# Turning the contexts between the thirds of the next pair's scores

## The reference

```python
# layer 0 (one head of width 8, its output repeated for 16 heads)
q = query @ Wq + bq; k = key @ Wk + bk; v = value @ Wv + bv
scores = jnp.einsum('bqd,bkd->bqk', q, k) / math.sqrt(HIDDEN)
scores = _layer_norm_scores(scores)          # mean and std over the 1500 keys
scores = scores + jnp.where(m, -1e-32, 0.0)
attn = jax.nn.softmax(scores, axis=-1)
head = jnp.einsum('bqk,bkd->bqd', attn, v)
return jnp.tile(head, (1, 1, NUM_HEADS)) @ Wout + bout
# layer 3 (layer norms of query, key and value around one head of width 128)
qk = jnp.einsum('bqd,bkd->bqk', q, k)
probs = jax.nn.softmax(qk / inv_scale_factor, axis=2)
out = jnp.einsum('bqk,bkd->bqd', probs, v)
return _layernorm(out, ln4_w, ln4_b)
```

## Time and profile before

| what | value |
|---|---|
| median of 3 runs | 3416.47 us (3416.21 to 3417.08) |
| the profiled execution's own time | 3413.9 us |
| its span in the profile | 3412.1 us |
| mean granted TensorE clock | 0.932 |
| TensorE busy | 3079.0 us, 90% of the span |
| layer 0: round 0 starts, last `out_turned` | 44.12 us, 208.67 us |
| layer 3: round 0 starts, last `out_turned` | 3087.48 us, 3254.01 us |

### The profile page before, as it was taken

The page is one execution under the profiler, slowest core; times in us unless marked ns, Lnnn a source line. Parts: engine busy times, 40 slices in busy tenths (PEclk is TensorE's granted clock), DMA queues, the critical chain, the costliest instruction groups (busy, mean ns, idle before and its releaser), DMA issues. The chain is left out here.

```text
span 3412.1 us, 74955 instructions
## 1 busy us (share of the span) xinstructions
PE 3079.0 (90%) x30282; PEld 2137.9 (63%) x30282; DVE 2292.5 (67%) x4268; ACT 1742.8 (51%) x2862; POOL 1869.8 (55%) x1048
## 2 busy tenths in 40 slices
PE   7979989999999999999979998899999995349969
PEld 5654556777777777777757777455555553236644
DVE  4555557777777777777644443799999985654455
ACT  4534325666656666665644454366666663114545
POOL 0004556777777777777642220588888872014427
PEclk9979988999999999999989999799999996559989
DMA  7730016776666667767514665433333321304600
GB/s 142 145 114 22 1 37 125 139 147 130 134 137 142 130 134 139 142 131 140 111 51 154 235 236 218 98 99 98 96 96 92 92 69 36 55 0 93 135 1 12
DMA packets 607380, 367.70 MB, mean 108 GB/s; under 512 B 462933, under 2 KB 566626, under 8 KB 606786
## 3 DMA queue, kind: packets, MB, share of 16 engines
q1 hardware_dynamic: 607042, 362.96, 46.1%
HBM read 174.41 MB, written 75.24 MB: 73 GB/s over the span
## 5 line engine op out<-in xcount | busy, mean ns | idle before, releaser
L1742 POOL TENSOR_TENSOR L_plo<-L_p,L_phi 128x1500 bf16<-128x1500 f32 x224 | 659.1, 2943 | 295.0 <-DVE L_phi L1819 295.0
L1699 ACT COPY L_ptlo<-L_lt 128x1536 bf16<-128x1536 bf16 x224 | 322.1, 1438 | 407.6 <-PE L_lt L1623 407.6
L2121 ACT ACTIVATE L2b_p<-L2b_score 125x448 f32<-125x448 f32 x768 | 378.7, 541 | 273.2 <-PE L2b_score L2034 272.0
L1637 PE MATMUL L_acc<-L_chi,L_pthi 125*128 125x128 bf16 x2688 | 462.1, 219 | 0.0
L1639 PE MATMUL L_acc<-L_chi,L_ptlo 125*128 125x128 bf16 x2688 | 461.4, 219 | 0.0
L1638 PE MATMUL L_acc<-L_clo,L_pthi 125*128 125x128 bf16 x2688 | 461.2, 219 | 0.0
L1808 DVE TENSOR_SCALAR_CACHE_REDUCE L_p<-L_score,L_cols 128x1500 f32<-128x1500 f32 x224 | 395.4, 1765 | 84.8 <-PE L_score L1615 84.6
L1819 DVE CAST L_phi<-L_p 128x1500 bf16<-128x1500 f32 x224 | 298.1, 1331 | 164.6 <-ACT L_p L1693 163.7
L1693 ACT ACTIVATE L_p<-L_p,L_least 128x1500 f32<-128x1500 f32 x224 | 346.5, 1547 | 67.0 <-DVE L_p L1808 63.1
L2164 POOL TENSOR_TENSOR L2b_psum<-L2b_p 125x896 f32<-125x896 f32 x128 | 266.8, 2084 | 131.0 <-ACT L2b_p L2121 128.6
L2191 DVE TENSOR_REDUCE L2b_max<-L2b_m 112x1 f32<-112x1000 f32 x256 | 300.7, 1195 | 17.2 <-PE L2b_m L2015 9.5
(11 more groups left out here) (635 smaller groups left out, 6890.8 us busy)
## 6 DMA issues: line engine op xcount, KB each, us to landing
L2b_kst<-L_keys SPq DMA_DIRECT2D x96, 375.0 KB, 5.6
L_ct<-L_ct SPq DMA_DIRECT2D x32, 768.0 KB
L2a_ct<-L_ct SPq DMA_DIRECT2D x32, 768.0 KB, 15.1
L_ctx<-dram_ctx SPq DMA_DIRECT2D x32, 750.0 KB
L_keys<-L2a_kout SPq DMA_DIRECT2D x32, 750.0 KB, 8.0
L_values<-L2a_vout SPq DMA_DIRECT2D x32, 750.0 KB
L2b_vin<-L_values SPq DMA_DIRECT2D x32, 750.0 KB
L0x_ctx<-dram_ctx SPq DMA_DIRECT2D x32, 672.0 KB
```

Source lines behind the costliest of these rows:

```text
L1637: pe.matmul(acc, w_hi[0:KP, t, :], v_hi[0:KP, t, :], start=(t == 0), stop=False)
L1699: act.copy(pt_lo[g % 2][:, :, :], lt_ps[:, 0:KT * 128].rearrange("p (t q) -> p t q", t=KT)).then_inc(lo_read, 1)
L1742: pool.tensor_tensor(p_lo[g % 2][:, :, 0:KP], probs[g % RP][:, :].rearrange("q (t k) -> q t k", t=KT), p_hi[g % 2][:, :, 0:KP], ALU.subtra ...
L2121: act.activation(probs[t % RP][:, half * 2 * GW:(half + 1) * 2 * GW], score_ps[half][0:KP, 0:2 * GW], ACT.Exp).then_inc(exp_done, 1)
```

## The change

On TensorE, groups 0, 1 and 2 of pair n+2 no longer stand behind the probabilities of pair n but one behind each third of the scores of pair n+1; group 3 stays where it was. On ScalarE, the copies of these three groups stand ahead of `output(n - 1)`. No instruction is added or taken away, and the order on VectorE, GpSimd and the transfer queue is as before.

```diff
-                def scores(n):
+                def scores(n, thirds):
                     if n >= P:
                         return
                     pe.wait_ge(tr_read, 2 * G * (n + 1))
-                    for i in range(3):
+                    for i in thirds:
                         wait(pe, exp_done, 3 * (n - 1) + i + 1 if n else 0)
...
                 for n in range(P):
-                    scores(n + 1)
+                    for i in range(3):
+                        scores(n + 1, (i,))
+                        turned_keys(n + 2, (i,))
                     if n >= 1:
                         out_turned(n - 1)
                     turned_probs(n, 0)
                     turned_probs(n, 1)
-                    turned_keys(n + 2, (0, 1, 2, 3))
+                    turned_keys(n + 2, (3,))
                     weighted(n, 0)
...
                 for n in range(P):
+                    keys(n + 2, (0, 1, 2))
                     if n >= 1:
                         output(n - 1)
-                    keys(n + 2, (0, 1, 2, 3))
+                    keys(n + 2, (3,))
                     exps(n + 1)
                     keys(n + 2, (4, 5))
```

More of the change, by code:

```diff
@@ L1015, in _ @@
                 pe.wait_ge(q_ready, NCH)
-                scores(0)
+                scores(0, range(3))
                 turned_keys(1, range(2 * G))
```

## The result

The changed kernel takes 3421.34 us (median of 13 runs, 3417.87 to 3428.22) against 3415.51 us for the kernel before in the same comparison (13 runs). The ratio is 1.0019 with a 95% interval of 1.001 to 1.0027: 6.5 us more, 3.4 to 9.2. The forecast was 3420.6, 4.1 us more than the 3416.5 it started from.

The account below looks back on a forecast made before the run. TensorE was taken to set the pace in both stages; layer 0's round +0.33 us and layer 3's -0.04, 14 times each, add 4.1 us to 3416.5, giving 3420.6 us; 8 in 10 between 3414.5 and 3426.0.

Parts of the forecast that it names:

- The copy waits: TensorE's third and fourth context groups wait for ScalarE's copies; 0.54 us a round (layer 0), 0.60 (layer 3), 16 us, go.
- Changeovers: Switching TensorE between half-array scores and whole-array transposes around two inserted context groups adds 0.51 us a round.
- S2: Last third of a round's scores on TensorE; forecast to start 3.05 us after the first third instead of 1.68.
- The lower bound: Changeovers cost only 0.10 us each way there, 0.20 for both inserted groups, if all else hides.
- the upper of 0.74: Changeovers cost 0.37 us each, as between weighted matmuls and transposes, 0.74 for both; rival's chance 0.16.
- The estimate of 0.66 us: Four added changeovers a round at 166 ns each instead of 0.51 us in all; forecast about 4 us higher.
- Layer 0's new wait on VectorE's copy: First weighted matmul waits for transposed probabilities, 3.30 us behind the scores' last third; TensorE idles 0.33 us a round.
- Layer 3 even: Layer 3's shorter VectorE chain adds practically no wait; round 10.69 us, 0.04 less than 10.73.
- Loads: Context transfers stay hidden, in layer 0 with 11.9 us where they had 14.3; late-load rival's chance 0.04.
- The 4.65 us: Stretch from a round's first weighted matmul to the next scores on TensorE, forecast unchanged in both layers.
- The rivals: Upper changeover price 3427.0 us, chance 0.16; no VectorE wait 3416.0, 0.10; hidden changeovers 3411.9, 0.06; late layer 0 loads 3431, 0.04.
- The sum: 14 rounds in each layer, 0.33 us longer in layer 0 and 0.04 shorter in layer 3: 4.1 us more.

Follow-up runs that it names:

- two groups ahead: Kernel before, with the first two groups of transposed contexts ahead of the first two groups of transposed probabilities on TensorE: 3401.69 us, ratio 0.9959.
- the single transpose between thirds: Kernel before, with only the one transpose `out_turned` moved from behind the scores' last third to behind the first: ratio 1.0029, 9.9 us slower.
- alone: The change made in layer 3 only, layer 0 keeping the order of the kernel before: ratio 1.0005.
- either new order on VectorE: Changed kernel, layer 0: first copy of transposed probabilities ahead of the aggregate, 1.0016; second copy also ahead of scale and bias, 1.0012 (ratios).
- one group between: Changed kernel, with one context group between the scores' first two thirds and two groups behind the last third: ratio 0.9983 against the kernel before.
- both copies first: Changed kernel, layer 0: VectorE's first copy of transposed probabilities ahead of the aggregate, the second ahead of scale and bias: ratio 1.0012.
- one block: On top of two groups ahead: all transposes together, then all weighted matmuls; ScalarE copies all six groups before the probabilities: 3381.86 us, ratio 0.9901.

## Why the prediction was right

- *The copy waits go.* Right, and sized right: 0.54 and 0.60 us a round read, 0.56 and 0.62 measured where nothing else changed (two groups ahead).
- *Changeovers.* Right: 0.51 us a round was forecast up to S2, and S2's place, 3.08 - 1.68 - 0.87, gives 0.53. The lower bound, weights hidden beneath the transposes, does not hold, nor does the upper of 0.74. One changeover there and back costs 0.29 us where one is taken out, so two cost 0.58: the 0.53 and about 0.05 behind S2. It is shown apart from everything else by the single transpose between thirds. The Trainium skill's rule (TensorEngine Tiling (Array Packing), Key Properties) that changing the tiling mode drains TensorE fits the gaps, but no run shows the drain itself. The estimate of 0.66 us from the 166 ns of the Trainium skill (TensorE: Matmul & The Clock Gate, Single matmul latency) is above what the rounds show.
- *Layer 0's new wait on VectorE's copy.* Right in place and size: 3.32 behind S2, 3.30 forecast, read off a round of the kernel before that turned no contexts. Round 11.05 for 11.00.
- *Layer 3 even.* 10.70 for 10.69, and alone not to be told from before.
- *Loads, ScalarE, the rest of the round.* The 4.65 us stayed. No group waited for a load in the rounds.
- *The rivals.* Without VectorE's wait the change would have been even, as layer 3 shows. What the prediction didn't see is that the wait is only the first of three in line behind the late S2; moving it away uncovers the next. Its claim that without this wait layer 0 would be even was not reached by either new order on VectorE (10.89 and 11.07 for 10.67).
- *The sum.* 4.1 forecast, 4.9 by the rounds, 6.5 (3.4 to 9.2) by the ratio. The 0.8 between the first two is 0.05 us a round in layer 0 and 0.01 in layer 3. The 1.6 between the last two is inside the interval. Round 0 of layer 0, which the sum took for a round like the others, was 1.7 us longer in the profiled execution, at the lower clock. Four of the five kernels with a changed order on ScalarE in layer 0 have such a first round (by 1.4 to 1.7 us: the changed one, one group between, both copies first, one block), and none of the five with the old order has. With one profiled execution of each it is not shown whether this belongs to the order or to chance.
- *Luck.* The forecast of 3420.6 lies 0.7 us from the measured median, closer than its sum deserves: it started from 3416.5, and the kernel before took 3415.51 in the comparison.

The argument was that the gain (16 us of waits) and the price (14 us of changeovers up to S2, about 1 us of slower starts behind it and 5 us of a new wait) are both small and real, and nearly cancel. The runs show each of the two alone: 0.9959 for the gain without the price, 1.0029 for a changeover without the gain.

## What to carry to other kernels

To cover a wait, first look for work of the same kind as its neighbours: here two groups of transposed probabilities, already in the round, covered the copies for nothing, while scores cost 0.29 us for each way there and back. When an engine's work is split by another's, ask who waits for its last part: a third that starts 1.4 us later moves every chain that hangs on it, and the chain with the least slack decides. And read starts of instructions, not busy time, where ends are drawn by a model.

## What was not expected of the hardware

- Transposes of probabilities straight behind scores start slower (0.98 us for eight against 0.87, 0.11 more) than those of contexts do there (1.07 us for eight against 1.02 as drawn, 0.05 more), so where the changeover falls matters by some 0.05 us.
- TensorE shows 20.00 of 20 us busy in a stage in which reordering the same instructions saved 11% of a round (10.70 to 9.54 us).
